# One program of four attention layers and four feed-forward layers: later loads in a head loop, semaphores cleared a stage later, weights loaded during a normalisation, four heads per step

## What is computed

```python
x = L0_attn_x
xn = _layernorm(x)      # layer 0: rotary attention, 16 heads, keys of 4; 8 experts, 2 per token
x = x + _L0_attn_ref(xn, ...) + _L0_ffn_ref(xn, ...)
xn = _layernorm(x)      # layer 1: causal attention with ALiBi, 16 heads of 16; Hadamard-turned MLP
x = x + _L1_attn_ref(xn, ...) + _L1_ffn_ref(xn, ...)
xn = _layernorm(x)      # layer 2: linear attention; 8 experts, 2 per token
x = x + _L2_attn_ref(xn, ...) + _L2_ffn_ref(xn, ...)
xn = _layernorm(x)      # layer 3: gated delta rule, 16 key heads, 32 value heads; looked-up MLP
x = x + _L3_attn_ref(xn, ...) + _L3_ffn_ref(xn, ...)
```

```python
scores = jnp.einsum('bhqd,bhkd->bhqk', q, k) / jnp.sqrt(jnp.float32(hd))
bias = slopes[:, None, None] * rel.astype(jnp.float32)
causal = jnp.where(rel > 0, -jnp.inf, 0.0).astype(jnp.float32)
attn = jax.nn.softmax(scores + (bias + causal)[None], axis=-1)
out = jnp.einsum('bhqk,bhkd->bhqd', attn, v)
return out.transpose(0, 2, 1, 3).reshape(B, S, D) @ wo + bo
```

## Time and profile before

| what | value |
|---|---|
| median of 3 runs | 2254.77 us (2252.49 to 2274.08) |
| time of the profiled execution | 2252.73 us |
| its span, first to last instruction | 2250.9 us |
| PE busy | 1980.6 us, 88% |
| DVE, ACT, POOL busy | 59%, 43%, 47% |
| mean granted TensorE clock | 0.93 of full speed |

### The profile page before, as it was taken

The page is one execution under the profiler, slowest core; times in us unless marked ns, Lnnn a source line. Parts: engine busy times, 40 slices in busy tenths (PEclk is TensorE's granted clock), DMA queues, the critical chain, the costliest instruction groups (busy, mean ns, idle before and its releaser), DMA issues. The chain is left out here.

```text
span 2250.9 us, 46075 instructions
## 1 busy us (share of the span) xinstructions
PE 1980.6 (88%) x16932; PEld 1239.8 (55%) x16932; DVE 1326.7 (59%) x2490; ACT 974.8 (43%) x2372; POOL 1050.5 (47%) x2230
## 2 busy tenths in 40 slices
PE   7879896789969779755999999999999999999878
PEld 5412564333324353332677677777777777777653
DVE  3534563695525427625777777777777777767421
ACT  3354232004411221123666566665566665666420
POOL 0530221000120004403788878887888887878710
PEclk8889998789979879867999999999999999999889
DMA  5043221100020011011322222222222222222200
GB/s 142 1 160 117 68 48 38 45 0 1 1 97 0 19 56 28 14 46 38 55 60 67 50 49 59 63 64 50 50 64 64 59 50 54 59 63 45 42 3 19
DMA packets 217275, 113.11 MB, mean 50 GB/s; under 512 B 138432, under 2 KB 197472, under 8 KB 216672
## 3 DMA queue, kind: packets, MB, share of 16 engines
q1 hardware_dynamic: 212976, 105.06, 18.4%
q0 software_dynamic: 4080, 5.15, 1.4%
HBM read 81.79 MB, written 31.54 MB: 50 GB/s over the span
## 5 line engine op out<-in xcount | busy, mean ns | idle before, releaser
L2444 POOL TENSOR_TENSOR a_term<-a_z,a_l 32x14 f32<-32x14 f32 (+6 forms) x896 | 341.8, 381 | 70.3
L2448 POOL TENSOR_TENSOR a_z<-a_z,a_term 32x14 f32<-32x14 f32 (+6 forms) x896 | 339.4, 379 | 70.2
L1995 PE MATMUL ps<-all_xn,a_w_qkv 128*128 128x512 f32 x512 | 252.2, 619 | 3.3 <-DVE a_at L2494 3.3
L2474 DVE SCALAR_TENSOR_TENSOR a_qkv<-a_raw,a_taps,a_qkv 128x1024 f32<-128x1024 f32 x192 | 246.9, 1286 | 6.2
L1559 POOL TENSOR_TENSOR all_x<-all_x,f_part_out 128x512 f32<-128x512 f32 x32 | 45.9, 1470 | 242.1 <-DVE f_part_out L1532 242.1
L2005 PE MATMUL ps<-a_w_z,all_xn 128*128 128x256 f32 x512 | 125.2, 389 | 16.8 <-ACT a_zs L2271 16.8
L2194 PE MATMUL ps<-a_out_t,a_w_out 128*128 128x256 f32 x512 | 132.9, 404 | 1.9 <-ACT a_out_t L2346 1.7
L1995 PEld LDWEIGHTS ps<-all_xn,a_w_qkv 128*128 128x128 f32 x512 | 90.9, 196 | 76.8 <-issue 69.8
L2267 ACT ACTIVATE a_raw<-ps 128x512 f32<-128x512 f32 x128 | 76.5, 598 | 118.2 <-PE ps L1995 117.5
L823 POOL DMA_INDIRECT f_sums<-a_y,a_xs x23 | 36.1, 1570 | 195.8 <-ACT a_y L773 193.0
L1152 POOL TENSOR_TENSOR a_heads<-a_mixed,a_recip 128x512 f32<-128x512 f32 x8 | 10.1, 1267 | 243.1 <-DVE a_recip L1218 243.1
(11 more groups left out here) (325 smaller groups left out, 4477.1 us busy)
## 6 DMA issues: line engine op xcount, KB each, us to landing
a_gc_rows<-a_g_dram SPq DMA_DIRECT2D x64, 256.0 KB, 4.9
a_v_dram<-a_v SPq DMA_DIRECT2D x64, 256.0 KB, 2.0
a_w<-in_f_w SPq DMA_DIRECT2D x24, 512.0 KB, 10.4
a_w_qkv<-in_a_w SPq DMA_DIRECT2D x16, 512.0 KB, 3.9
a_t_dram<-a_z SPq DMA_DIRECT2D x512, 8.0 KB
f_index_in<-in_f_index SPq DMA_DIRECT2D x2, 2144.0 KB, 11.0
a_w_z<-in_a_w SPq DMA_DIRECT2D x16, 256.0 KB, 2.8
a_w_out<-in_a_wo SPq DMA_DIRECT2D x16, 256.0 KB, 3.1
```

The source lines that it names most:

```text
L1995: mm = pe.matmul(ps[:, to, :], w_qkv[:, k, mt * P:(mt + 1) * P], xn[:, k, b * T:(b + 1) * T], start=k == 0, stop=k == KC - 1)
L2444: pool.tensor_tensor(term[:, 0:j, j + 1:], z[:, 0:j, j:j + 1].broadcast_to([HP, j, n]), rows[:, j:j + 1, j + 1:].broadcast_to([HP, j, n]), ...
L2448: pool.tensor_tensor(z[:, 0:j, j + 1:], z[:, 0:j, j + 1:], term[:, 0:j, j + 1:], ALU.add).then_inc(sub_step, 1)
L2474: dve.scalar_tensor_tensor(to, rows, tap, to, ALU.mult, ALU.add).then_inc(conv_ready if j == TAPS - 1 else conv_step, 1)
```

## The change

1. In a0, before the loads of expert e (0 to 3), SP waits for `probs_used` of 32, 48, 64 and 80, out of 128 in the head loop: that is the end of the 8th, 12th, 16th and 20th of its 32 groups.
2. `Stage.__exit__` opens no block. It puts the stage on a list; SP clears the semaphores of the stages on the list, in `Stage.clear_stale`, in its own instruction list of the next stage, behind that stage's loads. f3 has no such call, and nothing follows it.
3. The loads of a1, a2 and a3 become a function `load(sp)` that is handed to `layer_norm` of n1, n2 and n3 and issued there by SP at the start of the stage, before it clears semaphores. The normalisation is called from within the attention stage, after its weight buffers and before its other buffers are allocated.
4. In the second half of a1, `scores` and `mix` take both halves of a key block: four score matmuls and four value matmuls in a row. `mix(u - 1)` follows `scores(u)`. The three pairs of banks, the ring of six buffers, and all instructions of DVE, ACT and POOL stay as they are.

```diff
     def __exit__(self, *error):
-        if not error[0] and self.name != "all":
-            with self.nc.Block() as block:
-                @block.sync
-                def _(sp):
-                    for sem in self.sems:
-                        sp.sem_clear(sem)
         self.ctx.close()
+        if self.name != "all":
+            Stage.stale.append(self)
+
+    @staticmethod
+    def clear_stale(sp):
+        for stage in Stage.stale:
+            for sem in stage.sems:
+                sp.sem_clear(sem)
+            stage.sem_ctx.close()
+        Stage.stale.clear()
...
-def layer_norm(nc, name, ps, x, xn, mean_of, ident):
+def layer_norm(nc, name, ps, x, xn, mean_of, ident, ahead=None):
...
+            @block.sync
+            def _(sp):
+                if ahead is not None:
+                    ahead(sp)
+                Stage.clear_stale(sp)
...
                 route.fill(sp)
+                Stage.clear_stale(sp)
...
                 sp.wait_ge(roped, NT)
                 for e in range(E_ALL // 2):
+                    sp.wait_ge(probs_used, HG * (GROUPS // 4 + e * GROUPS // 8))
                     load_expert(e)
...
-def alibi_attention(nc, ps, d, x, xn):
+def alibi_attention(nc, ps, d, x, xn, norm):
...
+        def load(sp):
+            for to, of in ((wq, "a1_wq"), (wk, "a1_wk")):
+                sp.dma_start(to[:, :, :], d[of].rearrange("(k p) n -> p k n", p=P)).then_inc(qk_loaded, 16)
...
+        norm(load)
...
-                def scores(n):
-                    i, kt, half = pair(n)
-                    if n < SETS:
-                        pe.wait_ge(top_ready, ALL_UNITS - SETS + n + 1)
+                def scores(u):
+                    i, kt, _ = pair(2 * u)
+                    if u == 0:
+                        pe.wait_ge(top_ready, ALL_UNITS - SETS + 2)
+                    elif u == 1:
+                        pe.wait_ge(top_ready, ALL_UNITS)
+                        pe.wait_ge(probs_ready, 1)
                     else:
-                        pe.wait_ge(probs_ready, n - SETS + 1)
+                        pe.wait_ge(probs_ready, 2 * u + 1 - SETS + 1)
...
+                    for n in (2 * u, 2 * u + 1):
+                        for c in range(2):
+                            j = n % 2 * 2 + c
...
-                def mix(n):
-                    i, kt, half = pair(n)
-                    pe.wait_ge(probs_ready, n + 1)
+                def mix(u):
+                    i, kt, _ = pair(2 * u)
+                    pe.wait_ge(probs_ready, 2 * u + 2)
...
-                for n in range(ALL_UNITS + LAG):
-                    if n < ALL_UNITS:
-                        scores(n)
-                    if n >= LAG:
-                        mix(n - LAG)
-                    if n >= UNITS and n % UNITS == 5:
-                        sum_weights(n // UNITS - 1)
+                for u in range(ALL_UNITS // 2 + 1):
+                    if u < ALL_UNITS // 2:
+                        scores(u)
+                    if u >= 1:
+                        mix(u - 1)
+                    if u >= ST and u % ST == 2:
+                        sum_weights(u // ST - 1)
```

More of the change, by code:

```diff
@@ L1043, in turn_top @@
                     mm.then_inc(top_turned, 1)
-                def scores(n):
-                    i, kt, half = pair(n)
-                    if n < SETS:
-                        pe.wait_ge(top_ready, ALL_UNITS - SETS + n + 1)
-                    else:
-                        pe.wait_ge(probs_ready, n - SETS + 1)
-                    if n % UNITS == 0:
+                def scores(u):
[5 more added lines that the diff above has]
+                        pe.wait_ge(probs_ready, 1)
+                    else:
+                        pe.wait_ge(probs_ready, 2 * u + 1 - SETS + 1)
+                    if kt == 0:
                         pe.wait_ge(q_topped, i + 1)
[L1053 to L1058, removed]
-                def mix(n):
-                    i, kt, half = pair(n)
-                    pe.wait_ge(probs_ready, n + 1)
-                    if n % UNITS == 0:
+                    for n in (2 * u, 2 * u + 1):
+                        for c in range(2):
+                            j = n % 2 * 2 + c
+                            rows = slice(j * HP, (j + 1) * HP)
+                            mm = pe.matmul(ps[:, 2 * ((ALL_UNITS + n) % SETS) + c, 0:(ST - kt) * P],
+                                           k_all[rows, i, kt * P:(kt + 1) * P], q_all[rows, i, kt * P:],
+                                           start=True, stop=True)
+                        mm.then_inc(score_psum, 1)
+                def mix(u):
+                    i, kt, _ = pair(2 * u)
+                    pe.wait_ge(probs_ready, 2 * u + 2)
+                    if kt == 0:
                         if i < 2:
@@ L1067, in mix @@
                             pe.wait_ge(recip_ready, ST * (i - 1))
[L1068 to L1073, removed]
+                    for n in (2 * u, 2 * u + 1):
+                        for c in range(2):
+                            j = n % 2 * 2 + c
+                            mm = pe.matmul(ps[j * HP:(j + 1) * HP, Q_BANK + i % 2, kt * P:],
+                                           values[:, i // NG * ST + kt, i % NG * HG + j, :],
+                                           probs[:, n % RING, c, 0:(ST - kt) * P], start=kt == 0, stop=kt == ST - 1)
+                        mm.then_inc(mix_done, 1)
                 def sum_weights(i):
@@ L1247, in linear_attention, with load @@
         wo, bias, bo = s.buf("wo", [P, KC, C]), s.buf("bias", [P, 3, KC]), s.buf("bo", [P, KC])
+        loaded = s.sem("loaded")
+        def load(sp):
+            sp.dma_start(w[:, :, :, :], d["a2_w"].rearrange("q (k p) n -> p q k n", p=P)).then_inc(loaded, 16)
+            sp.dma_start(wo[:, :, :], d["a2_wo"].rearrange("(k p) n -> p k n", p=P)).then_inc(loaded, 16)
+            sp.dma_start(bias[:, :, :], d["a2_bias"]).then_inc(loaded, 16)
+            sp.dma_start(bo[:, :], d["a2_bo"]).then_inc(loaded, 16)
+        norm(load)
         ones = s.buf("ones", [P, T])
```

106 lines of the change are left out of this document (56 added, 50 removed).

## The result

The changed kernel takes 2191.7 us (median of 4 runs, 2188.9 to 2192.5), the kernel before 2253.6 (4 runs, 2249.1 to 2274.1): ratio 0.970, 95% interval 0.964 to 0.976. The forecast was 2177, range 2162 to 2202. The profiled execution went from 2252.7 to 2191.9 us, 60.9 less; 76.2 had been forecast. So 15.3 us of gain are missing, and the question is where.

The account below looks back on a forecast made before the run. Bounds: PE in a1's second half, idle clears between stages, DMA waits starting a1 to a3, a hole in a0. Gains 18.4 + 20.1 + 11.7 + 24 + 2 = 76.2 off 2252.7 gave 2176.5, stated as 2177; range 2162 to 2202.

Parts of the forecast that it names:

- Clears: Between stages: removing eleven blocks in which SP clears semaphores while engines idle gains 18.4 us, bounds 16 and 18.4.
- Loads in normalisations: Starts of a1, a2, a3: loads issued during n1, n2, n3 gain 7.0, 5.8, 7.3, sum 20.1 us, bounds 14 and 20.
- The fear that the DMAs slow a normalisation: n1, n2, n3: loads running beside the normalisation might slow it, costing at most 2 us each time.
- Weights at intervals: a0's head loop: spacing expert weights thins the crowd with scatters, removing most of a 13.7 us hole; gain 11.7, bounds -2, 13.7.
- the rival by bytes: a0: the stall goes by bytes, each weight burst stalls, that part gains nothing; 2188 us, chance 0.16.
- Four heads: a1's second half: four heads' matmuls run together, 9.3 us a tile, 75 us in place of 99; gain 24, bounds 0, 43.
- its rival: a1's second half: the clock falls, half the turns at half clock, a1 gains only 12 us; 2188 us, chance 0.18.
- the new loop has none over 0.7: a1's second half: argument against the clock falling, that PE's idle holes in the new loop stay within 0.7 us.
- Clock at f3: Start of f3: with the 4.9 us of clearing gone, PE keeps full clock; gain 2 us, bounds 0 and 2.
- Both rivals that had been priced at 2188: Clock falling in a1's second half (chance 0.18) and a0's stall going by bytes (0.16); together 2200 us.

Follow-up runs that it names:

- e10: Kernel before with only the later semaphore clearing (no block of its own): 2217.0 us, beside 2230.4 for the kernel before.
- e11: Changed kernel once more, unedited, in three rounds: 2193.8 us, ratio 0.971 to the kernel before.
- e6: Changed kernel, in a1's second half each pair of score matmuls waits for its own banks, for a tile's second key block alone: 2193.0 us.
- e5: Changed kernel, in a1's second half each pair of score matmuls waits for its own banks, for all key blocks: 2195.9 us.
- e1: Changed kernel with the weights of experts 0 to 3 asked for at once again, as before: 2184.5 us.
- e2: Changed kernel with one scatter in place of 16, experts working on unwritten rows: 2172.9 us.
- e4: Changed kernel with all 16 scatters issued only after the 12th group of a0's head loop: 2193.4 us.
- e7: Changed kernel with the 16 scatters issued in pairs spread over a0's head loop: 2179.1 us.
- e8: e7 with the weights of experts 0 to 3 also asked for at once: 2181.2 us.
- e12: Kernel of e9 once more, in three rounds: 2166.2 us, ratio 0.961 to the kernel before.
- e9: Changed kernel with scatters as in e7, DVE's look-up table wait later in a0, and, on top of e6, the first pair of a1's second key block issued twice: 2168.1 us.

## Why the prediction was right and wrong

- **Clears**: right, 18.4 for 18.4, and nothing comes back: the pair named as largest, a0's clears behind a1's loads in n1, leaves n1 at 13.9 us, 3.0 shorter than before.
- **Loads in normalisations**: right, each of the three starts to 0.1 us. The fear that the DMAs slow a normalisation didn't come true; n1 moved 338 GB/s from 382 to 384 and took 13.9 us, and in e10, with no load in it, 13.7. Left out of the sum was what the clock does from one execution to the next: n0, whose matmuls no kernel changes, takes 14.4 or 16.9 us, and a2 behind its start differs by 6 us between two executions of the changed kernel. That gave 3.2 us in a2 and 3.0 in n1 here and took 2.4 in n3.
- **Weights at intervals**: the step that failed is "at that time 6 MB of weights and POOL's 16 scatters are in flight together", read as a crowd that fewer weights would thin. The term should have been about 0 and not 11.7: a0 takes 356.9, 357.3, 358.3 and 359.2 us with the intervals (changed kernel, e11, e6, e5), 356.8 and 357.9 without (before, e1). Two things were in flight, and the prediction took the larger for the cause. It was the smaller one: 16 scatters, 2 MB, without which there is no stall (e2), and beside which the engines stall before any weight is asked for. Why they do so in all but e10 stays open. The row that could have told it was in the trace of before: at the end of the loop another 6 MB are in flight and PE goes on, as the prediction itself noted against the rival by bytes. The same argument speaks against the crowd's larger half.
- **Four heads**: the mechanism right, a term mis-sized, and its rival came true. The full-clock tile is 9.35 us (forecast 9.3), so the chain was priced well. The failing step is "the new loop has none over 0.7", said of idle time on PE; it has one of 1.39 in every tile. Between the scores of the first and the second key block of a tile there is only the value work of the last key block of the tile before, 0.43 us and not 1.07, and the turn is 3.0 us (570.52 to 573.51): the idle time is 3.0 - 1.14 - 0.43 = 1.4. The prediction's own numbers give 2.7 - 1.1 - 0.4 = 1.2; it had not been worked out key block by key block. Where the clock falls behind such a hole, the tile takes 1.0 us more, here five of six tiles, 5 us; the first tile began at half clock and took 17.8 us to its first sum, where e5's took 14.8, so 3 more. 75 and 8 are 83, measured 84.6, and 82.9 to 86.2 in the seven other executions of this code (e1 to e4, e7, e8, e11). The rival had said 12 us of gain; 14.5 were measured. The Trainium skill, TensorE: Matmul & The Clock Gate, section A second HAM failure mode: psum-queue depth-cycling (the prediction named the section before it), says that micro-idles between groups of matmuls make the clock swing. These runs agree, and add that holes of 0.4 us did not.
- **Clock at f3**: right, 2.2 us.
- **The whole**: 2177 against 2191.7. Both rivals that had been priced at 2188 hold in their sizes (a0 gains nothing, a1 12 to 14), which by the forecast's sum is 2200; what brings it back are 5.8 us that no term had, and a1's 2.5. The 5.8 are luck: by the same account e11, the same kernel, has 2.6 of them. The range held since it reached to both rivals together, not because the sum was right: of 35.7 us forecast for a0 and a1 14.4 came. There is a slip in the last step too: 2176.5 and the 2.0 to the median are 2178.5 and not 2177, which changes nothing here.

## What to carry to other kernels

Where two things are in flight during a stall, look for a place where each is alone before choosing the one to thin; here 16 GpSimd scatters, and not the 6 MB, were to be spread, and that was two lines and 10.6 us. After taking work off an engine, list its idle times between each pair of instructions of the new loop and not on average: one hole in the period can cost the clock. Before a gain in a stage is put down to a change, look at the same stage in other executions with the same code: a2 took 32.5 and 38.6 us in two executions of the changed kernel, and the stall 10.9 and 13.1.

## What the runs showed that had not been expected

- A burst of indirect DMAs from GpSimd, at 100 GB/s with the DMA engines 28% busy, can go with signals of PE that reach ACT and DVE 7 to 11 us late; in pairs 7 to 12 us apart (e7) the same scatters cost nothing, eight in a row 1.6, sixteen 10.9, 13.1, 13.4 and 13.4 (changed kernel, e11, e5, e6), and 13.7 and 13.8 with the weights beside them (before, e1), but nothing in e10. The Trainium skill, SBUF — State Buffer, section SBUF: two separate sides, says that a DMA can't be slowed by a compute operation nor the reverse. For DMAs that SP issues these runs agree (377 GB/s beside full pace in e8); beside a burst issued by GpSimd the engines stood still, in all runs but e10. That is no proof of contention at SBUF, since what they waited for was a signal.
- Issuing a pair of matmuls a second time, work thrown away, made a1 faster: 9.35 us a tile in place of 10.3 (e12 against e11). The pair also waits for its own banks there, but e6, which has that wait alone, lost the clock in three periods of six.
- A wait placed one operation too early on DVE cost 5 to 6 us of a0: PE stood behind a product that needed no table (a0 340.5 in e9 and 341.2 in e12, 346.3 in e7).
